# A post-norm transformer block on one core: three-part float32r products in place of float32, the first norm's factor and offset folded, three stacks instead of four

## What is computed

```python
Xn = (X - mu) * rsqrt(var + EPS) * ln_g + ln_b          # first norm, per row
Q, K, V = heads(Xn @ Wq + bq), heads(Xn @ Wk + bk), heads(Xn @ Wv + bv)   # 16 heads of 16
A = softmax(causal(Q K^T / 4))
x = layernorm(X + (A V) @ Wo + bo)
h = relu(x @ W1 + b1); alpha = softmax(h @ W2 + b2)      # 8 weights per row
out = sum_k alpha_k * (x @ V_k^T) @ U_k^T                # V_k, U_k of rank 64
y = layernorm(x + out)
```

## Time and profile before

| | |
|---|---|
| median of 3 runs | 463.79 us (462.13 to 464.18) |
| the profiled execution | 466.19 us, of it 464.3 us from first to last instruction |
| PE busy | 418.5 us (90%) |
| DVE busy | 310.2 us (67%) |
| ACT busy | 234.3 us (50%) |
| POOL busy | 73.3 us (16%) |
| mean granted clock of TensorE | 0.972 |

### The profile page before, as it was taken

One profiled execution on the slowest core, in us unless ns is written; L12 is line 12 of the kernel. 1 busy time (PEld: TensorE's weight loads), 2 busy tenths in 40 slices (PEclk: granted clock), 3 DMA queues, 4 the chain that ended last, 5 costly groups with the idle time before them and its releaser, 6 DMA issues.

```text
span 464.3 us, 7228 instructions
## 1 busy us (share of the span) xinstructions
PE 418.5 (90%) x2541; PEld 209.1 (45%) x2541; DVE 310.2 (67%) x805; ACT 234.3 (50%) x498; POOL 73.3 (16%) x108
## 2 busy tenths in 40 slices
PE   7898896998999989998899987998999989997892
PEld 3355342343344433466457733434334434356452
DVE  5427995888898694326666898688889661126076
ACT  6562553675667575442441453665776665530210
POOL 2132120143021010101130022024021010100000
PEclk9899898999999999999999999899999999999797
DMA  5056662260402000001763135053220000000011
GB/s 182 0 82 96 171 97 39 32 97 12 70 1 93 2 1 0 1 2 43 129 121 48 47 54 87 0 82 59 36 35 3 1 1 2 0 0 1 0 46 45
DMA packets 18435, 21.13 MB, mean 46 GB/s; under 512 B 4960, under 2 KB 11872, under 8 KB 18400
## 3 DMA queue, kind: packets, MB, share of 16 engines
q1 hardware_dynamic: 18349, 20.66, 23.6%
q10 hardware_dynamic: 51, 0.01, 0.0%
HBM read 5.79 MB, written 2.10 MB: 17 GB/s over the span
## 4 chain that ended last, share of the span: by engine, by line
PE 64%; DVE 19%; ACT 7%; SPq 4%; issue 3%; DMA 3%; POOL 1%; DVEq 0%; ACTq 0%
PE ps L766 23%; PE ps L868 13%; PE ps L848 12%; DVE mx L656 9%; PE ps L827 9%; PE ps L831 2%; ACT pr L559 2%; DMA stq<-mrow 2%; PE ps L760 2%; SPq L448 2%; SPq L449 2%; ACT stk L517 2%; DVE st L609 2%; DVE x L616 1%; PE ps L878 1%
## 5 line engine op out<-in xcount | busy, mean ns | idle before, releaser
L559 ACT ACTIVATE pr<-ps 128x512 f32<-128x512 f32 (+3 forms) x384 | 167.3, 495 | 111.3 <-PE ps L848 109.5
L656 DVE TENSOR_REDUCE mx<-ps 128x1 f32<-128x512 f32 (+3 forms) x304 | 182.1, 653 | 34.3 <-PE ps L831 25.5
L848 PE MATMUL ps<-stq,stk 99*128 99x512 bf16 (+3 forms) x384 | 118.5, 336 | 13.8 <-DMA stq<-mrow 8.7
L827 PE MATMUL ps<-stk,stq 96*128 96x512 bf16 (+3 forms) x384 | 115.4, 332 | 2.8 <-DVE mx L656 1.7
L868 PE MATMUL ps<-pr,va 128*32 128x512 f32 (+3 forms) x768 | 82.3, 501 | 0.0
L507 POOL TENSOR_SCALAR_AFFINE_SELECT pr<-pr 128x512 f32<-128x512 f32 x64 | 40.7, 636 | 261.0 <-ACT pr L559 261.0
L848 PEld LDWEIGHTS ps<-stq,stk 99*128 99x128 bf16 x384 | 35.0, 99 | 101.5 <-ACT pr L559 51.6
L831 PE MATMUL ps<-mask,ident_b 128*128 128x128 bf16 x256 | 50.3, 223 | 0.0
L827 PEld LDWEIGHTS ps<-stk,stq 96*128 96x128 bf16 x384 | 38.0, 99 | 21.1 <-issue 6.9
L766 PE MATMUL ps<-pr,w_qk 128*128 128x512 f32 x64 | 30.7, 625 | 2.3 <-ACT pr L526 2.3
L831 PEld LDWEIGHTS ps<-mask,ident_b 128*128 128x128 bf16 x256 | 25.6, 100 | 13.0 <-issue 3.9
(11 more groups left out here) (80 smaller groups left out, 346.7 us busy)
## 6 DMA issues: line engine op xcount, KB each, us to landing
stq<-qk_raw SPq DMA_DIRECT2D x32, 96.0 KB, 2.8
stk<-qk_raw SPq DMA_DIRECT2D x32, 96.0 KB, 2.8
x_in<-in_x SPq DMA_DIRECT2D x8, 256.0 KB, 3.6
...
```

What stands on the lines that cost most here:

```text
L559: nc.scalar.activation(probs(b, g, s)[:, j, q0 - c * CHUNK:], act_bank(ev)[:, q0 - c * CHUNK:], ACT.Exp, scale=DH ** -0.5).then_inc(s_act_ ...
L656: nc.vector.tensor_reduce(dst, src, AX.X, ALU.max).then_inc(s_dve_free, 1)
L827: last = nc.tensor.matmul(bank[:, i * w:(i + 1) * w], q[0:ROWS, t // TPC, j, tile(t % TPC)], k[0:ROWS, k0 // CHUNK, j, 0:w], start=True, s ...
L848: nc.tensor.matmul(bank[:, q0 - c * CHUNK:], stk[stack_of(b, g)][0:ROWS + PARTS, kt // TPC, j, tile(kt % TPC)], stq[stack_of(b, g)][0:ROWS ...
```

## The change

1. Products. `qk`, `v`, `h` and `vx` are made of three float32r products for each term instead of one float32 product. Both operands are split into a near part, written in float32r (ACT), and a far part, what is left (DVE). `part_products` adds near x near, far x near and near x far; far x far is left out. A `qk` or `h` now has six matmuls of 512 columns, a `vx` six of 512, a `v` twelve of 256. In `qk` and `h` PE waits for the far part of the rows only before its last two matmuls.
2. Splitting the rows. `xt` and `x1t` move from the ring that ACT frees to the one that DVE frees; ACT copies the near part, DVE subtracts it from the bank for the far part (new L691), 16 times in all. `xt` gets tensors of its own.
3. Splitting the weights. Eight new events `halve` in batch 0: ACT writes the near part of a weight half, DVE the far part. The weights are loaded whole into `o_t` and `x1`, which are free then; W1 and V come earlier than before.
4. The first norm's factor goes into the weights as they are split. Its offset times the weights is added to the biases: new events `shift` (four columns, eight float32 matmuls of one column, before the first `xt`) and `shift_v` (four of them, at step 8).
5. Start. ACT no longer waits for `cols` before its table and its fills, of which there are three. 12 idle products instead of 20. The second chunk's `ln1` of batch 0 is done in two pieces of two tiles, put behind the first and the second `qk`.
6. Three stacks. A group g uses stack g % 3 in batch 0, so group 3 takes stack 0 over from group 0; in batch 1 group 3 takes over the stack of that batch's group 0 in the same way. `stack` (2, 1) stands at step 13 now, and `stack` (3, 0) at step 17, in both batches.
7. `va` is packed 17 numbers to a head instead of 32; the operand of a value product is 32 columns as before.

```diff
-STACKS = 4
+STACKS = 3
...
-    order = ([("load", 0)] + [("ln1", 0, c * TPC, TPC) for c in range(C)] + begin(0, 0) + [("stack", 0, 1, 0)]
-             + begin(0, 1)[:parts] + vs[0][:2])
+    halves = [("halve", 0, name, k) for name in ("qk", "v", "1", "vt") for k in range(parts)]
+    first = begin(0, 0)
+    order = ([("load", 0), ("ln1", 0, 0, TPC), ("shift", 0)] + halves[:parts] + first[:parts] + first[parts:parts + 1]
+             + [("ln1", 0, TPC, TPC // 2)] + first[parts + 1:parts + 2] + [("ln1", 0, TPC + TPC // 2, TPC // 2)] + first[parts + 2:]
+             + [("stack", 0, 1, 0)] + halves[parts:2 * parts] + begin(0, 1)[:parts] + vs[0][:2])
...
+            beside[8] = [("shift_v", 0)]
             beside[9] = [("fold", 0)]
         for k, t in zip((13, 17, 21, 25), pairs):
             beside[k] = [("bo", b, t)]
-        for k, g, c in ((2, 2, 0), (4, 1, 1), (11, 3, 0), (15, 2, 1), (22, 3, 1)):
+        for k, g, c in ((2, 2, 0), (4, 1, 1), (13, 2, 1), (17, 3, 0), (22, 3, 1)):
             beside[k] = [("stack", b, g, c)] + beside.get(k, [])
...
-            order += qks + woven(opening[:at_split], vs[0][2:3]) + [opening[at_split]] + vs[0][3:] + opening[at_split + 1:]
+            order += woven(qks[:-1], halves[2 * parts:]) + qks[-1:] + woven(opening[:at_split], vs[0][2:3]) + [opening[at_split]] + vs[0][3:] + opening[at_split + 1:]
...
-        w_qk = sb("w_qk", [P, KC, 2, D])
-        w_v = sb("w_v", [P, KC, D])
+        w_qk = sb("w_qk", [P, 2, KC, 2, D], F32R)
+        w_v = sb("w_v", [P, 2, KC, D], F32R)
         w_o = sb("w_o", [P, KC, D])
-        w_1 = sb("w_1", [P, KC, D])
+        w_1 = sb("w_1", [P, 2, KC, D], F32R)
         w_2 = sb("w_2", [P, KC, E])
-        v_t = sb("v_t", [P, KC, ER])
+        v_t = sb("v_t", [P, 2, KC, ER], F32R)
...
+        xt_parts = sb("xt_parts", [P, 2, C, KC, CHUNK], F32R)
...
-        x1_t = sb("x1_t", [P, KC, CHUNK])
+        x1_t = sb("x1_t", [P, 2, KC, CHUNK], F32R)
...
+        whole_qk = o_t[:].rearrange("p k (w d) -> p k w d", w=2)
+        whole_1, whole_v = (x1[:, t:t + 2].rearrange("p t d -> p (t d)").rearrange("p (k d) -> p k d", k=KC) for t in (0, 6))
+        whole_vt = x1[:, 2:6].rearrange("p t d -> p (t d)").rearrange("p (k d) -> p k d", k=KC)
+        split_weights = {"qk": (whole_qk, w_qk), "v": (whole_v, w_v), "1": (whole_1, w_1), "vt": (whole_vt, v_t)}
...
-        n_act = count("xt", "v", "score", "ot", "x1t", "h", "avt")
-        n_dve = count("qk", "fold", "max", "rows", "turn", "r1", "lg", "vx", "u")
+        n_act = count("v", "score", "ot", "h", "avt")
+        n_dve = count("xt", "shift", "shift_v", "qk", "fold", "max", "rows", "turn", "r1", "lg", "x1t", "vx", "u")
+        n_near, n_halve = count("xt", "x1t"), count("halve")
...
+                        weight(whole_1, w1, "1")
+                        weight(whole_vt, vt, "vt")
...
-                        weight(w_1[:], w1, "1")
-                        weight(v_t[:], vt, "vt")
...
-            act.wait_ge(s_cols, 16)
-            nc.scalar.activation(le[:, 0, 0, 0:1], cols[:, 0, 0:1], ACT.Exp)
             act.wait_ge(s_one_minus, 1)
+            nc.scalar.activation(le[:, 0, 0, 0:1], minus[:, 0:1], ACT.Exp)
             for i in range(STACKS):
                 nc.scalar.activation(stk[i][ROWS:ROWS + PARTS].rearrange("p c h s -> p (c h s)").bitcast(F32),
                                      minus[ROWS:ROWS + PARTS, :].bitcast(F32).to_broadcast([PARTS, C * HPG * CHUNK // 2]),
                                      ACT.Copy).then_inc(s_minus, 1)
+            act.wait_ge(s_cols, 16)
...
+                if kind == "halve":
+                    _, _, name, k = ev
+                    whole, split = split_weights[name]
+                    act.wait_ge(s_w[name], 32 if name == "qk" else 16)
+                    gain = cols[:, 0, k:k + 1] if name in ("qk", "v") else 1.0
+                    nc.scalar.activation(split[:, 0, k], whole[:, k], ACT.Copy if gain == 1.0 else ACT.Identity,
+                                         scale=gain).then_inc(s_weight_near, 1)
+                if kind in ("xt", "x1t"):
+                    _, _, c, k = ev
+                    act.wait_ge(s_dve_full, n_dve[ev])
+                    nc.scalar.activation(xt[0][:, c, k, :] if kind == "xt" else x1_t[:, 0, k, :], dve_bank(ev),
+                                         ACT.Copy).then_inc(s_near, 1)
...
+                if kind == "halve":
+                    _, _, name, k = ev
+                    whole, split = split_weights[name]
+                    dve.wait_ge(s_weight_near, n_halve[ev])
+                    near = split[:, 0, k].bitcast(F32)
+                    if name in ("qk", "v"):
+                        ins = nc.vector.scalar_tensor_tensor(split[:, 1, k], whole[:, k], cols[:, 0, k:k + 1], near,
+                                                             ALU.mult, ALU.subtract)
+                    else:
+                        ins = nc.vector.tensor_tensor(split[:, 1, k], whole[:, k], near, ALU.subtract)
+                    ins.then_inc(s_weight_far, 1)
+                if kind in ("xt", "x1t"):
+                    _, _, c, k = ev
+                    near, far = (p[:, c, k, :] for p in xt) if kind == "xt" else (x1_t[:, i, k, :] for i in range(2))
+                    dve.wait_ge(s_near, n_near[ev])
+                    nc.vector.tensor_tensor(far, dve_bank(ev), near.bitcast(F32), ALU.subtract).then_inc(s_dve_free, 1)
+                if kind == "shift":
+                    dve.wait_ge(s_dve_full, n_dve[ev])
+                    dve.wait_ge(s_cols, 16)
+                    nc.vector.tensor_tensor(cols[:, 2:4, :], dve_bank(ev)[:, 0:2 * KC].rearrange("p (w m) -> p w m", w=2),
+                                            cols[:, 2:4, :], ALU.add).then_inc(s_dve_free, 1)
+                if kind == "shift_v":
+                    dve.wait_ge(s_dve_full, n_dve[ev])
+                    dve.wait_ge(s_bv, 16 * KC)
+                    nc.vector.tensor_tensor(bv[:], dve_bank(ev)[:, 0:KC], bv[:], ALU.add).then_inc(s_dve_free, 1)
...
+            def part_products(out_, lhs, rhs, which, n, start=False, stop=False):
+                terms = [(i, j, k) for i, j in which for k in range(n)]
+                for i, j, k in terms:
+                    last = nc.tensor.matmul(out_, lhs(i, k), rhs(j, k), start=start and (i, j, k) == terms[0],
+                                            stop=stop and (i, j, k) == terms[-1])
+                return last
...
-            turn_over(20)
+            turn_over(12)
...
+                if kind in ("shift", "shift_v"):
+                    bank = take_dve(ev)
+                    pe.wait_ge(s_cols, 16)
+                    if kind == "shift":
+                        weights("qk", b, 32)
+                        columns = [(whole_qk[:, :, w], m) for w in range(2) for m in range(KC)]
+                    else:
+                        weights("v", b)
+                        columns = [(whole_v, m) for m in range(KC)]
+                    for i, (whole, m) in enumerate(columns):
+                        last = product(bank[:, i:i + 1], lambda k: whole[:, k, tile(m)], lambda k: cols[:, 1, k:k + 1], KC)
+                    last.then_inc(s_dve_full, 1)
                 if kind == "qk":
                     _, _, m, c, w = ev
                     bank = take_dve(ev)
-                    weights("qk", b, 32)
-                    pe.wait_ge(s_act_free, n_act["xt", b, c, KC - 1])
-                    product(bank, lambda k: w_qk[:, k, w, tile(m)], lambda k: xt[:, c, k, :], KC).then_inc(s_dve_full, 1)
+                    if b == 0:
+                        pe.wait_ge(s_weight_far, n_halve["halve", 0, "qk", KC - 1])
+                    sides = lambda i, k: w_qk[:, i, k, w, tile(m)], lambda j, k: xt[j][:, c, k, :]
+                    pe.wait_ge(s_near, n_near["xt", b, c, KC - 1])
+                    part_products(bank, *sides, ((0, 0), (1, 0)), KC, start=True)
+                    pe.wait_ge(s_dve_free, n_dve["xt", b, c, KC - 1])
+                    part_products(bank, *sides, ((0, 1),), KC, stop=True).then_inc(s_dve_full, 1)
...
                 if kind == "v":
                     t = ev[2]
                     bank = take_act(ev)
-                    weights("v", b)
+                    if b == 0:
+                        pe.wait_ge(s_weight_far, n_halve["halve", 0, "v", KC - 1])
                     for i in range(2):
                         c, n = divmod(t + i, TPC)
-                        last = product(bank[:, i * D:(i + 1) * D], lambda k: xt[:, c, k, tile(n)], lambda k: w_v[:, k, :], KC)
+                        last = part_products(bank[:, i * D:(i + 1) * D], lambda i, k: xt[i][:, c, k, tile(n)],
+                                             lambda j, k: w_v[:, j, k, :], ((0, 0), (0, 1), (1, 0)), KC, start=True, stop=True)```

```

(1 more changed line is left out.)

69 lines of the change are left out of this document (41 added, 28 removed).

## The result

The change takes 491.09 us (median of 4 runs, 489.61 to 492.19) beside 463.99 us of the kernel before in the same job: a ratio of 1.058, 95% interval 1.053 to 1.064. It is slower, as forecast, but by 27 us and not by 11; 475 us was predicted, and 491 lies outside the range of 463 to 486. The profiled execution took 490.38 us, where 477.5 was predicted for it.

The account below looks back on a forecast made before the run. PE was taken as the bound (418.5 of 464.3 us busy, 64% of the chain), though not everywhere. Products -9.9, stacks +15.8, `shift_v` +0.9 and start +4.5 made +11.3 on 463.8: 475 us, range 463 to 486.

Parts of the forecast that it names:

- the start: Up to the first maximum: DVE's longer queue moves it from 36.52 to 41.0 us, 4.5 us lost.
- the products: `qk`, `v`, `h` and `vx`: 0.42 us saved per event; 36 events worth 15.1 us at most, 9.9 us gained.
- Three stacks: 15.8 us lost: First `max` of group 3, both batches: PE idles 7.2 us awaiting the reloaded stack; 7.9 us lost each, 15.8 together.
- I take 0.22: One float32r matmul of 512 columns takes 0.22 us, like bf16; six take 1.32 us instead of 1.74.
- Rival 3: In the products, a weight load of 0.19 us tops each float32r matmul, cancelling the cut: 485 us; chance 0.04.
- The transposes' move to the other ring: `xt` and `x1t` go to the other ring: costed at nothing, ACT copying as much as before.
- the first `qk` ends at 13.6, with PE at full clock: At the start: the first product ends at 13.6 us, and DVE's high part and rest are done by 15.1.
- a piece 4.0 us: At the start: each two-tile piece of the second chunk's `ln1` takes DVE 4.0 us, 2.6 of it small steps.
- shift_v 0.9 us: Where PE and DVE are both full: eight records of one column at 0.11 us each, 0.9 us lost.
- The two waits for far parts: Batch 0's `h` and the turn of the batches: PE waits for DVE's subtractions, losing 1.8 and 2.1 us of gain.

Follow-up runs that it names:

- e1: The kernel before with three stacks instead of four and nothing else of the change: 477.65 us, ratio 1.025 to the kernel before.
- e5: The kernel before, four stacks, with ACT's first table load and four fills no longer waiting for `cols`: 462.52 us, ratio 0.996 to the kernel before.
- e3: The changed kernel with the second chunk's `ln1` of batch 0 in one piece, behind the first two `xt`: 482.66 us, ratio 1.036 to the kernel before.
- e8: The changed kernel without `shift_v`, and with the third norm of batch 0's first chunk behind the second chunk's transposes: 489.78 us, ratio 1.055 to the kernel before.
- e10: The kernel before plus early fills and float32r `h` and `vx` (459.38 us), with batch 1's first norm moved behind batch 0's first `x1t` far part: 456.53 us.

## Why the prediction was wrong

The direction held, and the largest term too. Three steps failed: the start (4.5 us predicted, 9.9 measured), the products (9.9 us of gain predicted, 5.8 arrived) and `shift_v` (0.9 us predicted, 2 to 3 measured). By its steps:

- **"Three stacks: 15.8 us lost"** was right, and not by luck: 16.7 after the change, 15.6 in e1 on the same lines. Place, chain, idle time (6.9 to 8.2 us against 7.2), the low clock behind and what comes back (0.8 us in e1 against 0.6) are as told. The 8.15 us after the change, against 6.93 in the other batch, go with one issue on SP's queue that took 1.78 us instead of 0.59. e1's expectation, not the prediction, forgot that one fill less gives 3.9 us at the start, a gain that four stacks can have as well (e5).
- **"I take 0.22"** for a float32r matmul failed: it is 0.25 to 0.27. The bf16 row it was taken from has the same count of columns, and 0.04 us more on six matmuls is more than half of the 0.42 us saved. With 0.15 to 0.26 an event, the 36 events are worth 5 to 9 us at most, not 15.1; of the 9.9 forecast, 5.8 arrived, and part of that was the tail's clock. The weights' loads, mean 0.19 to 0.23 us in the profile's groups, fill nearly all of that pitch; whether they set it was not tested. Rival 3, that they come on top (0.22 + 0.19), is refuted by the pitch. The rows it was argued from are of matmuls 96 and 99 rows high, not of full height; the float32r ones are. The transposes' move to the other ring, put at nothing, was not run by itself.
- **The start, "4.5 us lost"**, was 9.9. The second chunk was normed at 28.6, not 23.9, and all behind it moved by the same 5 us: `v` at 32.92 instead of 27.9, the first `max` at 46.4 instead of 41.0. Of these 5 us, 3.0 are the first products: "the first `qk` ends at 13.6, with PE at full clock", but it starts at 13.64, at the low clock (0.50 from 10 to 16 us, through the transposes and the five idle products too), and DVE's first rest comes at 17.33, not at 14.4. The other 1.8 are "a piece 4.0 us": 5.1 and 4.9, because in each piece one tiny step on DVE lasted until POOL's subtraction ended. The small steps themselves were sized rightly (4.1 without that), and POOL beside DVE stands nowhere in the sum. The structure was as told; e3 shows that the cut in two, with its place behind the first rest, costs 6 to 8 us against the norm in one piece.
- **"shift_v 0.9 us"** was 3.1 by e8 and 2.0 as a mean over all traces. Its instructions were priced at full clock, but the stretch they stand in is at the low one (1.8 us for the eight), and the clock stays low for longer behind them.
- **The two waits for far parts** came: 2.21 us before the last two matmuls of the `h` at 196.94, and 0.99 us at 251.04, at the turn. The first was priced at 1.8 us with the saving lost; e10 gained 3.8 where it stood, 1.7 of it by the clock, which the sum had left out there.

The misses of the start, the products, the stretch of `shift_v` and the stalls are 5.4, 4.1, 2.5 and 0.9 us, together the 12.9 between 11.3 and 24.2. Most of them are costs read at the full clock that were paid at the low one, or a neighbour's row taken at its value; POOL beside DVE is a third kind. The range did not cover it: the start went beyond its bound of 7, and `shift_v` had no bound at all; the gain and the stalls stayed inside theirs.
